# Expert weights brought to fixed places by DMA, tile by tile, in a routed feed-forward stage

## The reference

```
scores = x @ Wg + bg                       # 8 experts
topk_vals, topk_idx = top_k(scores, 2)
gates = softmax(topk_vals)
h = gelu(x @ W1[e] + b1[e])                # 256 -> 384, for each chosen expert e
y = h @ W2[e] + b2[e]                      # 384 -> 256
out = sum over the two chosen e of gates * y
```

## Time and profile before

| | us |
|---|---|
| median of 3 runs | 478.45 |
| lowest and highest run | 476.68, 479.40 |
| span of the profiled execution | 494.5 |

### The profile page before, as it was taken

The page is one execution under the profiler, slowest core; times in us unless marked ns, Lnnn a source line. Parts: engine busy times, 40 slices in busy tenths (PEclk is TensorE's granted clock), DMA queues, the critical chain, the costliest instruction groups (busy, mean ns, idle before and its releaser), DMA issues.

```text
span 494.5 us, 8809 instructions
## 1 busy us (share of the span) xinstructions
PE 375.3 (76%) x2955; PEld 254.4 (51%) x2955; DVE 310.4 (63%) x652; ACT 184.4 (37%) x360; POOL 201.3 (41%) x152
## 2 busy tenths in 40 slices
PE   0999869999899998897966791145987888888523
PEld 0646545566466652543455471035765667667422
DVE  3656363389933896689988678953444454445365
ACT  1343634344342440241414646105433444335223
POOL 3203443133331320065545456551655655555422
PEclk9999999999999998899866896557999998989856
DMA  8900000000000700002270224211222222222195
GB/s 243 373 2 2 0 1 1 1 0 2 0 1 2 212 2 2 2 0 64 65 201 13 64 65 148 85 54 33 76 76 87 76 76 76 77 80 72 66 303 207
DMA packets 27050, 36.00 MB, mean 73 GB/s; under 512 B 7328, under 2 KB 22560, under 8 KB 26880
## 3 DMA queue, kind: packets, MB, share of 16 engines
q1 hardware_dynamic: 20880, 22.98, 14.6%
q0 software_dynamic: 3952, 10.37, 7.2%
q10 hardware_dynamic: 2176, 2.10, 1.3%
HBM read 26.13 MB, written 9.31 MB: 72 GB/s over the span
## 4 chain that ended last, share of the span: by engine, by line
PE 42%; DVE 29%; issue 11%; ACT 5%; another core or an unknown queue 4%; DMA 4%; POOL 1%; SPq 1%; ACTq 0%; DVEq 0%
PE ps L1338 17%; PE ps L1583 8%; PE ps L1569 8%; PE ps L1441 3%; DVE sm L898 3%; DVE u_h L908 2%; DVE t L1217 2%; DMA cols<-in_L_conv_bv_dram 2%; DVE tiles L1164 2%; PE ps L1557 1%; ACT late L774 1%; DMA l<-expert_rows_dram 1%; DVE work L971 1%; PE ps L1493 1%
## 5 line engine op out<-in xcount | busy, mean ns | idle before, releaser
L1569 PE MATMUL ps<-late,l 128*128 128x128 f16 x702 | 97.0, 230 | 16.1 <-issue 9.7
L1583 PE MATMUL ps<-l,late 128*128 x351 | 87.1, 283 | 7.8 <-issue 6.4
L1569 PEld LDWEIGHTS ps<-late,l 128*128 x702 | 63.9, 103 | 30.2 <-issue 22.8
L479 POOL TENSOR_TENSOR tiles<-tiles 128x1024 f16<-128x1024 f32 x16 | 34.5, 2158 | 94.3 <-ACT tiles L704 94.3
L559 POOL DMA_INDIRECT expert_rows_dram<-late,idx x39 | 38.8, 994 | 53.7 <-DVE late L1207 48.6
L774 ACT ACTIVATE late<-ps,b_sb 128x128 f32<-128x128 f32 x117 | 34.4, 365 | 67.9 <-remote 47.3
L1441 PE MATMUL ps<-u_h,tiles 128*128 128x256 f16 x256 | 44.5, 272 | 9.0 <-DVE u_l L909 9.0
L1207 DVE TENSOR_TENSOR late<-ps,qk 128x256 f32<-128x256 f32 x39 | 16.6, 424 | 52.0 <-remote 36.3
L1338 PE MATMUL ps<-l 128*128 128x512 f16 x192 | 44.2, 380 | 0.1
L555 POOL DMA_INDIRECT late<-token_rows_dram,idx x39 | 37.9, 972 | 14.8 <-issue 11.3
L1583 PEld LDWEIGHTS ps<-l,late 128*128 128x128 f16 x351 | 34.6, 99 | 15.2 <-issue 8.3
(11 more groups left out here) (304 smaller groups left out, 780.6 us busy)
## 6 DMA issues: line engine op xcount, KB each, us to landing
prep<-in_L_ffn_W_dram SPq DMA_DIRECT2D x16, 384.0 KB, 3.3
l<-expert_rows_dram SPq DMA_DIRECT2D x16, 256.0 KB, 5.8
l<-in_x_dram SPq DMA_DIRECT2D x4, 512.0 KB, 8.6
token_rows_dram<-val SPq DMA_DIRECT2D x2, 1024.0 KB, 4.6
l<-in_inv_f_dram SPq DMA_DIRECT2D x1, 1536.0 KB, 6.2
out_dram<-l SPq DMA_DIRECT2D x3, 512.0 KB, 2.8
qk<-in_L_ffn_b_dram SPq DMA_DIRECT2D x8, 128.0 KB, 3.8
fwd_hi_sb<-in_fwd_hi_dram SPq DMA_DIRECT2D x1, 768.0 KB, 12.2
```

The costliest lines, as they stand in the source:

```text
L479: PL.tensor_tensor(Pt[1][:, n % 2, :], prob[:, n % 2, :], Pt[0][:, n % 2, :], ALU.subtract).then_inc(p_low, 1)
L1569: last = PE.matmul(psh[s % 2][:, m * P:(m + 1) * P], experts[:, bass.ds(e, 1), o:o + P].rearrange("p a c -> p (a c)"), xT[:, s % 2, (r * C ...
L1583: last = PE.matmul(psy[s % 2], hh[l][:, s % 3, m * P:(m + 1) * P], experts[:, bass.ds(e, 1), o:o + C].rearrange("p a c -> p (a c)"), start ...
```

## The change

PE no longer reads `experts`. SP, for each tile, loads the tile's expert number from `where`, and copies that expert's W1 half (high and low, 1536 fp16 columns, 3 KB per partition, 384 KB) and then its W2 half (the same size) by DMA from `experts`, at an address held in a register, into one of four fixed places for each: `first_w[s % 4]` and `second_w[s % 4]`. These places are the memory of the Fourier tables `fwd` and `inv`, which are no longer used by then. PE waits for the landing (`first_in`, `second_in`) before a tile's hidden and before its result matmuls, whose operands are now fixed addresses. SP waits for `hid_full` before it overwrites a first place and for `y_full` before it overwrites a second one. `read_where` is gone.

```diff
+        first_w = [fwd[i // 2][:, (i % 2) * 2 * CC * H:(i % 2 + 1) * 2 * CC * H] for i in range(4)]
+        second_w = [inv[i // 2][:, (i % 2) * 2 * CC * H:(i % 2 + 1) * 2 * CC * H] for i in range(4)]
...
+            sp.wait_ge(where_ready, 1)
+            sp.wait_ge(we_low, 2 * E)
+            for s in range(TILES):
+                e = sp.value_load(where[0:1, s:s + 1], min_val=0, max_val=E - 1)
+                if s >= 4:
+                    sp.wait_ge(hid_full, s - 3)
+                sp.dma_start(first_w[s % 4], experts[:, bass.ds(e, 1), 0:2 * CC * H].rearrange("p a c -> p (a c)")).then_inc(first_in[s % 4], 16)
+                if s >= 4:
+                    sp.wait_ge(y_full, s - 3)
+                sp.dma_start(second_w[s % 4], experts[:, bass.ds(e, 1), 2 * CC * H:].rearrange("p a c -> p (a c)")).then_inc(second_in[s % 4], 16)
...
-                e = at_expert[s % 16]
+                pe.wait_ge(first_in[s % 4], 16 * (s // 4 + 1))
                 for m in range(HC):
...
-                        last = PE.matmul(psh[s % 2][:, m * P:(m + 1) * P], experts[:, bass.ds(e, 1), o:o + P].rearrange("p a c -> p (a c)"),
+                        last = PE.matmul(psh[s % 2][:, m * P:(m + 1) * P], first_w[s % 4][:, o:o + P],
...
-                e = at_expert[s % 16]
                 pe.wait_ge(hid_low, s + 1)
+                pe.wait_ge(second_in[s % 4], 16 * (s // 4 + 1))
...
-                    o = (2 + r) * CC * H + m * C
-                    last = PE.matmul(psy[s % 2], hh[l][:, s % 3, m * P:(m + 1) * P], experts[:, bass.ds(e, 1), o:o + C].rearrange("p a c -> p (a c)"),
+                    o = r * CC * H + m * C
+                    last = PE.matmul(psy[s % 2], hh[l][:, s % 3, m * P:(m + 1) * P], second_w[s % 4][:, o:o + C],
...
-            pe.wait_ge(where_ready, 1)
-            pe.wait_ge(we_low, 2 * E)
-            read_where(0)
...
-                    if n == 4 and 0 < i < TILES and i % 8 == 0:
-                        read_where(i)
```

More of the change, by code:

```diff
@@ L366, in conv_attn_moe_kernel @@
         scattered = [sem(f"scattered{k}") for k in range(4)]
+        first_in = [sem(f"first_in{k}") for k in range(4)]
+        second_in = [sem(f"second_in{k}") for k in range(4)]
         x_turned, x_taken, hid_full, gelu_done, hid_high, hid_low, y_full, y_taken = (
@@ L1587, in results @@
                     yield
[L1589 to L1596, removed]
             dst = fill("UW")
```

## The result

| | before | after |
|---|---|---|
| median of the runs, us | 478.91 | 522.86 |
| lowest to highest, us | 476.68 to 479.40 | 521.62 to 525.01 |
| ratio, 95% interval | | 1.096, 1.089 to 1.102 |
| span of the profiled execution, us | 494.5 | 522.2 |

The change costs 44 us. Ratios are those of undisturbed executions, so they need not be those of the medians. The direction and the mechanism were forecast, but the cost is twice the 22 us of the forecast. That the time still lies in the range of 480 to 532 us is due to the width that the rivals gave the range, not to the sum.

A forecast was written before the change was run, and what follows sets the result against it. PE was taken to bound the expert stage through register issue, with POOL close behind. Iterations going from 2.88 to 3.5 us, 34 x (3.5 - 2.88) = 21 us, plus 1 for the start, on 478.45 gave 500.5 us; range 480 to 532.

The forecast's parts named there:

- What bounds the stage, and what can be won: Expert stage: PE bounds it, its excess being register issue; POOL's 2.57 us a tile is the floor, saving at most 10.5 us.
- The stalls read as none of the kernel's: PE's periodic stalls in the expert stage, 16 to 18 us in all, left out, giving 2.88 us an iteration instead of 3.35.
- A cost of profiling: Reason given for PE's stalls of 1.2 us or so about every 6.8 us: they come from profiling the execution.
- The order of SP's waits gives one iteration of lead, and two iterations take L + X: SP's next first copy stands behind its wait for `y_full`; an iteration takes (4.8 + 2.15) / 2 = 3.5 us.
- L: Time from the end of one PE iteration to the landing of the next first copy: 4.8 us, ends 3.6 and 6.85.
- X: Time from a first copy's landing to the end of the PE iteration that needs it: 2.15 us.
- The near end of 2.4 us for the landing: Lower end for a first copy from issue to landing, assuming a source without DRAM's delay: 2.4 us.
- The landing's 0.3 us for everything else on the DMA engines: Added to a first copy's 3.2 us landing for gathers and scatters, the second copy being about out of the way.
- The start: Before iteration 4 of the expert stage: eight copies queue up and less backlog is left, costing 1 us.
- The tail doesn't change: End of the kernel, behind the expert stage's loop: no change in time, so no term in the sum.
- The falling clock: PE, busy 63%, drops to the lower clock level, 4.0 us an iteration: 517 us, 510 to 532; chance 0.18.
- Half rate: SP's SBUF to SBUF copies run at half the rate, 4.3 to 5.7 us a tile: 527 to 575 us; chance 0.10.

## Why the prediction was half right

- *What bounds the stage, and what can be won.* Right. Register work was PE's pace and POOL the floor: 2.59 us an iteration without it, and some 8 us in all against at most 10.5.
- *The stalls read as none of the kernel's.* Right, and with it the 2.88 us an iteration; the undisturbed trace has 2.83. It adds 34 x 0.05 = 1.7 us to the cost. "A cost of profiling" was wrong as a reason: other executions were profiled without any.
- *The order of SP's waits gives one iteration of lead, and two iterations take L + X.* Right. The landing releases PE in 26 of 33 rounds, a landing shorter by 0.68 us shortens the iteration by about half of that, and the iteration falls from 3.94 to 3.34 and 3.09 us with the order of the queue alone.
- *The size of L and X.* This is the step that failed, and the largest part of what was missing. L was put at 4.8 us and is 5.25: 1.43 to the issue for 1.2 to 1.35 (SP's issue with an address in a register is 0.49 us and not 0.37), and 3.82 to the landing for 3.5. Three parts of the time to the issue were estimates: the wake, put at 0.05, took 0.12 in the trace of the change, the load of `where` with its register work and check 0.48 at the medians for 0.55, the address 0.05 for 0.1. The near end of 2.4 us for the landing stood on no row, and no run isolates a delay of DRAM: the fastest first copy of the change landed in 3.0, as the fastest load did. X was put at 2.15 at full clock and is 2.33 in the 20 rounds at full clock, of which 0.14 from the landing to the first matmul had no term; in 6 rounds with slowed matmuls it is 3.35, so 2.56 on the mean. Half of 0.45 + 0.41 is 0.43 us: 3.94 for 3.5, 34 x 0.44 = 15 us of the 22 that were missing. Some 6 to 8 of the 15 are the clock's, by the estimates under the rivals.
- *The landing's 0.3 us for everything else on the DMA engines.* The prediction had the second copy about out of the way. Nine of the 33 first copies did land in 3.0 us, 1.2 us behind their second copy. But of the eleven issued within 3.2 us of the first copy of the round before none landed under 3.4 us (mean 4.2), and the nine issued more than 4.5 us behind it took 3.4 on the mean. Issued only 0.62 us behind the second copy they took 4.44. So at 1.2 us it seems to be the traffic of the round before that the sum lacked; no run isolates it.
- *The start.* From the first turn to that of iteration 4 it takes 10.96 us in place of 7.85: 3 us for the 1 assumed.
- *"The tail doesn't change".* Wrong. Behind turn 38 the changed kernel takes 42.1 us in place of 39.2: the last hidden matmuls wait for first copies too. PE is done with the results of the last tile 12.2 us after that turn, and 9.8 in the kernel before.
- *The sum of these.* 15 + 1.7 + 2 + 2.9 = 21.6 of the 22 us. The first turn itself is at 335.3 and 334.5 in the two traces of the change and at 328.9 in both of the kernel before, but at 326.1 to 337.8 in the variants, none of which touches what lies ahead. The sum closes without it; what moves it is open.
- *The rivals.* The falling clock (0.18, 510 to 532) took place in part: 0.92 in the stage, and the time lies in its range. Between 397 and 414 us, at a clock of 1.00, iterations took 3.7 us, so that some 34 x 0.23 = 8 us are the clock's; the rounds with slowed matmuls give 6 x 1.0 = 6 us. Both are estimates, and no run isolates the share. Half rate is excluded: the copies moved 26.15 MB in 51.3% of 133.87 us, 381 GB/s while busy, so 2.1 us a tile for the 2.2 taken. It is more than the 328 GB/s of SP's loads back to back, the way the prediction leaned; whether the larger pieces or the source does it, no run isolates.

## What to carry to other kernels

A ring of four places gives four tiles of lead only if nothing in the issuing queue stands ahead of the transfer with a later condition: write down, for each transfer, the last thing that its queue must pass, and the iteration in which it is needed. In a loop that closes through a transfer, everything that the queue does in a round, other transfers included, is in the loop, and a transfer issued sooner behind another one may land no sooner (here 0.65 us sooner at the issue, 0.62 us longer to the landing). And where a profiled span is longer than the runs by several per cent, read an undisturbed trace before taking per-iteration times from it.

## What was not expected of the hardware

- PE's load of eight words of SBUF into its registers took 0.6 us at the median (1.32 once), and 1.44 (up to 2.93) while the DMA engines were busy 0.94 of the time; five loads in each trace.
- A first copy within SBUF, 384 KB, landed in 3.0 us at best in the trace of the change, no sooner than the same size from DRAM (3.0); the least in any trace here is 2.6, with W1 alone by copies. In the change a copy cost the 16 DMA engines 1.03 us: 51.3% of 133.87 us for some 66.5 copies.
- SP took 0.49 us to issue a DMA with its source in a register, against 0.37 for one with a fixed address.
- With twelve small matmuls per iteration without any use, PE's granted clock was 0.96 in the stage, and 0.92 in both traces without them.
